# Matrix squarings drained by ScalarE, a gate product and a normalisation moved on GpSimd

## What is computed

```python
ada = silu(c) @ W_ada + b_ada
shift_msa, scale_msa, gate_msa, shift_mlp, scale_mlp, gate_mlp = split(ada, 6)
x = x + gate_msa * attention(modulate(layernorm(x), shift_msa, scale_msa))   # 16 heads of 9
x = x + gate_mlp * (gelu(modulate(layernorm(x), ...) @ W_fc1 + b_fc1) @ W_fc2 + b_fc2)

U, _ = qr(P)                    # P is 144 x 64
A = skew(silu(c) @ W.T + b)     # 64 x 64, one per sequence
R = expm(A)
z = x @ U
x = x + (z @ R - z) @ U.T
```

## Time and profile before

| | |
|---|---|
| median of 3 runs | 378.99 us |
| the profiled execution's own time | 378.52 us |
| its span, first to last instruction | 376.4 us |
| TensorE matmuls busy | 311.6 us, 83% |
| VectorE busy | 245.7 us, 65% |
| ScalarE busy | 144.5 us, 38% |
| GpSimd busy | 118.4 us, 31% |
| mean granted TensorE clock | 0.919 of full speed |

### The profile page before, as it was taken

How to read it: one execution, slowest core, us unless ns; L and a number is a source line. 1 busy time by engine, 2 the same in 40 slices (tenths; PEclk the granted TensorE clock), 3 DMA queues, 4 the chain that set the end, 5 groups by cost and what they waited for, 6 DMA issues and landing times.

```text
span 376.4 us, 7579 instructions
## 1 busy us (share of the span) xinstructions
PE 311.6 (83%) x2645; PEld 187.5 (50%) x2645; DVE 245.7 (65%) x763; ACT 144.5 (38%) x262; POOL 118.4 (31%) x299
## 2 busy tenths in 40 slices
PE   2888966888989789798888887989659999996686
PEld 1333423444444445465554554566536666665456
DVE  6857577676867868879889698764513455545533
ACT  2111112587674734445556364643103233231010
POOL 5812604207016383244270422122160333300000
PEclk9999999998998967989999999999958999997855
DMA  4923321123621212212113000000000000000004
GB/s 120 285 59 98 90 57 31 54 70 73 178 46 46 86 42 58 68 31 65 54 49 93 7 3 3 3 2 0 2 2 0 2 0 2 1 0 2 0 0 125
DMA packets 20202, 17.95 MB, mean 48 GB/s; under 512 B 3524, under 2 KB 18005, under 8 KB 20040
## 3 DMA queue, kind: packets, MB, share of 16 engines
q1 hardware_dynamic: 19556, 16.34, 15.8%
q10 hardware_dynamic: 610, 1.14, 1.0%
HBM read 12.28 MB, written 4.81 MB: 45 GB/s over the span
## 4 chain that ended last, share of the span: by engine, by line
PE 57%; DVE 23%; issue 6%; SPq 4%; ACT 3%; POOL 1%; DMA 0%; DVEq 0%; ACTq 0%; POOLq 0%
DVE nm L914 11%; PE pst L264 10%; PE m L483 6%; PE m L642 6%; PE pst L265 5%; PE ps L449 5%; PE m L286 3%; DVE gp L722 3%; PE m L270 3%; PE pst L470 3%; PE pst L381 3%; SPq L254 2%; DVE gm L723 2%; PE m L264 2%; PE pst L654 2%
## 5 line engine op out<-in xcount | busy, mean ns | idle before, releaser
L914 DVE TENSOR_REDUCE nm<-ps 128x2 f32<-128x512 f32 x128 | 87.6, 688 | 35.3 <-PE ps L449 31.2
L1146 ACT ACTIVATE pex<-pst 128x1024 f32<-128x1024 f32 x64 | 65.6, 1025 | 30.2 <-PE pst L470 29.1
L449 PE MATMUL ps<-ks,qs 54*128 54x256 bf16 x256 | 28.9, 305 | 22.6 <-DVE nm L914 21.9
L751 DVE TENSOR_SCALAR pm<-m 64x1 f32<-64x1 f32 x64 | 13.6, 212 | 45.8 <-PE m L286 45.4
L483 PE MATMUL m<-pex,ve 128*32 128x256 f32 x512 | 37.8, 417 | 0.0
L1458 POOL TENSOR_TENSOR xin<-xin,res 128x288 f32<-128x288 f32 x16 | 12.7, 791 | 71.0 <-DVE res L943 71.0
L270 PE MATMUL m<-gm,ident 64*64 64x65 f32 x126 | 24.4, 282 | 6.9 <-DVE gm L723 3.9
L449 PEld LDWEIGHTS ps<-ks,qs 54*128 54x128 bf16 x256 | 10.9, 101 | 36.3 <-issue 31.2
L286 PE MATMUL m<-qst,ident 64*64 64x64 f32 (+42 forms) x128 | 19.8, 234 | 11.1 <-DVE qst L757 11.1
L470 PE MATMUL pst<-qs,ks 56*128 56x256 bf16 x256 | 27.0, 290 | 1.8 <-DMA qs<-nmT 1.0
L270 PEld LDWEIGHTS m<-gm,ident 64*64 64x64 f32 x126 | 14.3, 159 | 26.9 <-issue 19.6
(11 more groups left out here) (248 smaller groups left out, 574.2 us busy)
## 6 DMA issues: line engine op xcount, KB each, us to landing
scr_qk<-parts SPq DMA_DIRECT2D x24, 144.0 KB, 2.0
qs<-scr_qk SPq DMA_DIRECT2D x96, 36.0 KB
ks<-scr_qk SPq DMA_DIRECT2D x72, 36.0 KB
gates<-scr_ada SPq DMA_DIRECT2D x2, 576.0 KB, 6.3
out_dram<-xin SPq DMA_DIRECT2D x8, 144.0 KB, 1.9
wr<-in_L_cond_W_dram SPq DMA_DIRECT2D x1, 1134.0 KB
xin<-in_x_dram SPq DMA_DIRECT2D x1, 864.0 KB, 5.2
ks<-scr_qk ACTq DMA_DIRECT2D x24, 36.0 KB
```

Of the source, the lines that this page charges most:

```text
L449: ins = mm(ps[e][:, L * i:L * i + L], qs[64 * e:64 * e + KS, b % 3, 2 * g + i, 128 * lt:128 * lt + 128], ks[64 * e:64 * e + KS, b % 3, 2 * ...
L914: nc.vector.tensor_reduce(nm[:, lt, e, 2 * g:2 * g + 2], ps[e][:, :].rearrange("p (h l) -> p h l", h=2), AX.X, ALU.max, negate=True).then_ ...
L1146: nc.scalar.activation(pex[:, n % 4, :, :], pst[0][:, :, :], ACT.Exp, scale=ATT_SCALE).then_inc(s("exp_done"), 1)
```

## The change

Four edits.

- A squaring becomes (E + 2I) E. GpSimd adds 2I, a constant tile, to `ef` and writes `ef2`, which lies in the memory of `qq`; TensorE multiplies `ef2` with `ef`; ScalarE copies the product over `ef`. VectorE has no part in it.
- The squares stand in other slots: (3,7), then slots 0, 3, 6 of turns 4 to 7; the last one stands in turn 1 of the MLP, ahead of the transposition into the same bank.
- The attention's projection is copied out of PSUM by ScalarE (`projected`) in slot 0, for sequences 0 to 5, and GpSimd multiplies it with the gate ahead of its addition to x. Sequences 6 and 7 stay as they were.
- GpSimd normalises input t + 4 at the end of turn t, behind the split, instead of input t + 3 at the start of turn t behind the shift.

```diff
-            for n in ((7,) if t == EXPM else (3, 5, 7) if t < B - 1 else (3, 4, 5, 7)):
+            for n in (7,) if t == EXPM else (0, 3, 6):
                 SQUARES[t, n] = len(SQUARES)
...
             def square(n, bank):
-                pe.wait_ge(s("ef_ready"), n + 1)
+                pe.wait_ge(s("ef2_ready"), n + 1)
...
-                            last = mm(m[half, at:at + R], ef[half, p, 1 - e, :], ef[half, p, e, :], start=True, stop=True)
+                            last = mm(m[half, at:at + R], ef2[half, p, 1 - e, :], ef[half, p, e, :], start=True, stop=True)
...
                     chain(mlp_steps(t, 5))
+                if t == 1:
+                    square(SQUARINGS - 1, 5)
                 if t >= 0 and real(t + 2):
                     transpose_h(B + t + 2, 5)
...
-            def squared(n):
-                m = await_fill(dve, "square", n)
-                ins = nc.vector.scalar_tensor_tensor(out=ef_flat, in0=ef_flat, scalar=2.0, in1=m[:, :], op0=ALU.mult, op1=ALU.add)
-                drained(ins, "square", n)
-                await_drain(dve, "square", n)
-                dve.sem_inc(s("ef_ready"), 1)
...
-                    if n == 0 and real(t - 2):
-                        gated("proj", t - 2, 0, res[:, :, :])
...
-                    if (t, n) in SQUARES:
-                        squared(SQUARES[t, n])
...
+            def squared(n):
+                drained(nc.scalar.copy(ef_flat, await_fill(act, "square", n)[:, :]), "square", n)
+
+            def projected(b):
+                m = await_fill(act, "proj", b)
+                if b:
+                    act.wait_ge(s("x1_ready"), b)
+                drained(nc.scalar.copy(res[:, :, :].rearrange("p t c -> p (t c)"), m[:, 0:LT * C]), "proj", b)
...
+                    if n == 0 and real(t - 2):
+                        projected(t - 2)
...
                     if n == 6 and real(t + 3):
                         evac_qk("qk01", t + 3, 0, 2)
+                    if (t, n) in SQUARES:
+                        squared(SQUARES[t, n])
...
+                if t == 1:
+                    squared(SQUARINGS - 1)
                 if real(t + 2):
                     evac_hT(B + t + 2)
...
+            def gated(b):
+                await_drain(pool, "proj", b)
+                if b == 0:
+                    pool.wait_ge(s("gates_loaded"), 32)
+                then(nc.gpsimd.tensor_tensor(res[:, :, :], res[:, :, :], gates[:, 0, b:b + 1, :].to_broadcast([128, LT, C]), ALU.mult))
+                xb = xin[:, LT * b:LT * b + LT, :]
+                nc.gpsimd.tensor_tensor(xb, xb, res[:, :, :], ALU.add).then_inc(s("x1_ready"), 1)
+
+            def plus_two(n):
+                if n:
+                    await_drain(pool, "square", n - 1)
+                else:
+                    await_drain(pool, "e0", 0)
+                nc.gpsimd.tensor_tensor(ef2[:, :, :, :].rearrange("p b e n -> p (b e) n"), ef[:, :, :, :].rearrange("p b e n -> p (b e) n"),
+                                        two_i[:, :].unsqueeze(1).to_broadcast([2 * R, 2 * BP, R]), ALU.add).then_inc(s("ef2_ready"), 1)
+
+            def plus_two_after(t, n):
+                if (t, n) in SQUARES and SQUARES[t, n] + 1 < SQUARINGS:
+                    plus_two(SQUARES[t, n] + 1)
...
             for t in range(-1, B):
                 if t > 0:
                     shift(t, 1)
-                if t >= 0 and t + 3 < B + 2:
-                    normalise(t + 3)
+                plus_two_after(t, 0)
                 if real(t - 2):
-                    added("proj", t - 2, res[:, :, :], "x1_ready")
+                    gated(t - 2)
+                plus_two_after(t, 3)
                 if t >= 0 and real(t + 1):
                     shift(t + 1, 0)
                 if t == BASIS_TURN:
                     basis_norms()
                 if real(t - 2):
                     mlp_deviations(t - 2)
+                if t == EXPM:
+                    plus_two(0)
+                plus_two_after(t, 6)
                 if t == 2:
                     weight_parts(1, wfc1_b, "mlp_loaded", 96, slice(3 * C, 3 * C + FF))
                 if real(t + 3):
                     split(t + 3)
+                plus_two_after(t, 7)
+                if t + 4 < B + 2:
+                    normalise(t + 4)
```

More of the change, by code:

```diff
@@ L68, in cond_seq_program @@
         below = sb("below", [R, R])
+        two_i = sb("two_i", [2 * R, R])
         onesb = sb("onesb", [3 * H2 * 2, L], BF16)
@@ L114, in cond_seq_program @@
         ef = sb("ef", [2 * R, BP, 2, R])
+        ef2 = qq
         efs = sb("efs", [R, B, R])
@@ L241, in cond_seq_program @@
         for t in range(EXPM, B):
-            for n in ((7,) if t == EXPM else (3, 5, 7) if t < B - 1 else (3, 4, 5, 7)):
+            for n in (7,) if t == EXPM else (0, 3, 6):
                 SQUARES[t, n] = len(SQUARES)
-        assert len(SQUARES) == SQUARINGS
+        assert len(SQUARES) == SQUARINGS - 1
         TURNED = [(0, 7), (1, 6), (2, 5), (3, 5), (4, 5), (6, 5), (7, 5), (7, 6)]
@@ L874, in exponential_of_scaled @@
                 drained(ins, "e0", 0)
-                await_drain(dve, "e0", 0)
-                dve.sem_inc(s("ef_ready"), 1)
-            def squared(n):
-                m = await_fill(dve, "square", n)
-                ins = nc.vector.scalar_tensor_tensor(out=ef_flat, in0=ef_flat, scalar=2.0, in1=m[:, :], op0=ALU.mult, op1=ALU.add)
-                drained(ins, "square", n)
-                await_drain(dve, "square", n)
-                dve.sem_inc(s("ef_ready"), 1)
             def signs():
@@ L894, in signed_exponential @@
             def signed_exponential():
+                await_drain(dve, "square", SQUARINGS - 1)
                 for e in range(2):
@@ L940, in gated @@
                     dve.wait_ge(s("x1_ready" if which == 0 else "x2_ready"), b)
-                elif which == 0:
-                    dve.wait_ge(s("gates_loaded"), 32)
                 ins = nc.vector.tensor_tensor(to, m[:, 0:LT * C].rearrange("p (t c) -> p t c", t=LT),
@@ L1165, in channels @@
                 drained(nc.scalar.copy(oTb[:, :], m[0:CB + 1, L:2 * L]), "oc", t)
+            ef_flat = ef[:, :, :, :].rearrange("p b e n -> p (b e n)")
+            def squared(n):
[5 more added lines that the diff above has]
+                drained(nc.scalar.copy(res[:, :, :].rearrange("p t c -> p (t c)"), m[:, 0:LT * C]), "proj", b)
             def turn_a(t):
@@ L1509, in _ @@
                                         pattern=[[0, BP], [-1, R]], channel_multiplier=1).then_inc(s("half_ready"), 1)
+            nc.gpsimd.memset(two_i[:, :], 0.0).then_inc(s("two_ready"), 1)
+            for i in range(2):
+                pool.wait_ge(s("two_ready"), i + 1)
+                nc.gpsimd.affine_select(out=two_i[:, :], in_=two_i[:, :], compare_op=ALU.not_equal, fill=2.0, base=-R * i,
+                                        pattern=[[-1, R]], channel_multiplier=1).then_inc(s("two_ready"), 1)
+            pool.wait_ge(s("two_ready"), 3)
             for t in range(-1, B):
```

## The result

The kernel after takes 396.31 us (median of 4 runs, 393.43 to 398.15) against 379.15 (378.2 to 379.45) for the kernel before on the same chip: ratio 1.0463, 95% interval 1.0411 to 1.0515. It is slower, as forecast, but by 17.2 us where 8.2 were forecast, and 396.3 lies above the range. The profiled execution took 398.15 us, 396.4 of it span, at a mean granted clock of 0.888 (0.919 before). Some executions of a kernel take over 1.5% longer than its fastest, at a lower mean clock; the medians here are over all executions, the ratios leave those out.

What follows compares the result with a forecast made beforehand. Neither TensorE nor VectorE was full; GpSimd's margins ahead of TensorE's shift transposition (1.56 to 2.22 us) decide. Terms 2.4 + 2.4 + 2.9 + 1.6 - 1.0 - 1.2 - 0.8 + 1.95 = +8.2 us gave 387; range 380 to 392.5.

Steps and rivals of the forecast that it cites:

- 2.4 + 2.4 + 2.9 + 1.6 = 9.3: TensorE's waits for GpSimd's delayed shift, in us: ends of turns 0 to 2 together, then of turns 3, 4 and 5.
- about 10%: Expected share of GpSimd in the chain of work that ended last, up from 1%.
- The gate's product: Moving six gate products from VectorE to GpSimd was credited no gain, and their time on GpSimd was taken as hidden.
- The wait of 0.86 for nmT: Slot 5 of turn 4: the square's wait for bank 5, held by the shift's copy, was to be gone.
- Rival B: VectorE held off by GpSimd's two-input additions and products: +3 us, 390; chance 0.12.
- Rivals C: C: half of the turn-end costs vanish in existing waits, 9.3 becomes 4.7: 382.5 us; chance 0.12.
- rival D: TensorE reaches the shift's transposition no earlier than GpSimd delivers, stalls vanish, only the squares' terms stand: -2.5, 376.5 us; chance 0.10.
- rival A: TensorE's stops in slot 1 bring three more falls of the granted clock: +4 us, 391; chance 0.14.
- Term 1.95: Last square in the MLP's turn 1: 1.08 us of its own plus a wait of 0.87 for its copy.
- Terms -1.0, -1.2 and -0.8: Gains in us from the attention's squares in their new slots, in turns 4, 6 and 7.
- -1.4 for turn 5: Gain in us of turn 5 from the squares, counted only if its end has no stall.

Runs made afterwards that it cites:

- gate_only: The kernel before with the gate's product alone moved (ScalarE copies the projection, GpSimd multiplies): 377.93 us, ratio 1.0015 to the kernel before.
- norm_back: The kernel after with GpSimd's normalisation put back behind the shift, all else as changed: 384.53 us, ratio 1.0155 to the kernel before.
- last_early: norm_back with the last square one MLP turn sooner, in turn 0: 380.12 us, ratio 1.0038 to the kernel before.
- fill: The kernel after with twelve unread matmuls ahead of the wait for the shift in slot 1, 84 in all: 387.86 us, ratio 1.0279 to the kernel before.
- slots_only: The kernel before with only the squares' slots new, VectorE still combining: 381.15 us, ratio 1.0084.
- last_early_warm: last_early with the filler matmuls of warm: 372.8 us, ratio 0.9862 to the kernel before.
- warm: The kernel before with 36 unread matmuls in the MLP's turn 0 and six per chain gap in its last two turns: 372.05 us, ratio 0.9869.
- squares_only: The kernel before with the squares alone changed (ScalarE's copy, GpSimd's addition, new slots): 384.65 us, ratio 1.0107.
- after_warm: The kernel after with all fillers, those of fill and warm and eight in the MLP's turn 1: 384.4 us, ratio 1.015 to the kernel before.
- norm_only: The kernel before with GpSimd's normalisation alone moved ahead of the next shift: 389.03 us against 378.22, one of 4 runs at 382.06.

## Why the prediction was off by half

**Right.** GpSimd's order was the cause, and the place was as forecast: six waits in slot 1, 10.3 us in sum where 2.4 + 2.4 + 2.9 + 1.6 = 9.3 was the forecast, the longest 2.81. That the sums agree is partly luck: the first three waits make 5.1 us for 2.4, the last three 5.2 for 6.9. The chain's share of GpSimd came out at 12% for "about 10%". The gate's product costs nothing (gate_only). The wait of 0.86 for nmT is gone, slot 5 of turn 4 went from 4.19 to 2.12 us. Rival B fell: L728's mean did not move. Rivals C and D fell too: six waits of 10.3 us stand there, and undoing the normalisation gives 11.8 us, so nothing was absorbed. An addition takes 1.268 us, inside its bounds. (The Trainium skill, "GPSIMD Engine Reference", section "Elementwise — side-by-side cycle accounting", scaled down to 512 elements, would have given an estimate of 1.12; the measurement decides.)

**The step that failed: the granted clock taken as it was.** The sum prices waits and moved work and puts the clock at nothing. In the profiles TensorE's rest grew by 8.6 us, close to the forecast's 8.2; the other 11.4 us are its same 2645 matmuls taking longer. Of the 11.4, 3.6 go with the normalisation (after to norm_back), 3.5 with the last square (to last_early), and 4.3 stay with the squares in the attention. That fill gets 8.4 us back net, though GpSimd is no sooner in the place shown, says the same. This is rival A, to which the forecast gave 0.14, argued from turns 4 to 7 having run at 1.00 in the kernel before. That was evidence from one execution of a stream without these stops. Its price was also read too low: turn 2 of the earlier trace rows touches three falls and not two, and the low clock grew by 27.8 us, not by three falls of 4. (The Trainium skill, "TensorE: Matmul & The Clock Gate", section "HAM oscillation", says that waits for DMA which recur in a loop bring the low clock back each time. Here the waits are for GpSimd, and three of the six have a fall at them and three have not.)

**The turn ends: the mechanism right, the size nearly.** The forecast's kernel without the stops is rival D's, 376.5; with them 387.2. That prices the normalisation at 10.7 us, and norm_back measures 11.8. In the profiles the parts are off in opposite directions: 7.5 us of rest where 10.7 were priced, and 3.6 of slower matmuls that had no term.

**The last square: sized at less than half.** Term 1.95, measured 4.4 (norm_back to last_early). Its own time and its copy, 1.14 and 0.69, were in the sum; the second wait of 0.68 and the low clock behind both were not.

**The squares in the attention: the wrong sign, and the largest miss.** Terms -1.0, -1.2 and -0.8, with rival D's -1.4 for turn 5 -4.4; measured +1.6 in all by last_early, which has the other two costs taken out. The step that failed is the one that priced slots 5 to 7 and took the squares of slot 0 as free. In turn 4 the gain of slot 5 was larger than forecast (2.06 for 1.1), but the square in slot 0 pays its own 1.08 and a wait of 1.04 for an addition queued behind the split, and slots 6 and 7 together lost 1.07. The -1.2 of turn 6 became +2.1: slot 0 lost 1.9, and slot 6 ran at the low clock. Why it fell there is open, since slots_only has the longer wait and no fall. Turn 7's -0.8 came, as -0.6. Nor is it the clock alone: last_early_warm is no faster than warm.

Against the forecast, then: 1.1 us short on the turn ends, 2.4 on the last square, 6.0 on the squares in the attention. The three measured steps, 11.8 + 4.4 + 1.6 = 17.8, are one chain of differences from the kernel after to the kernel before. That they come to the measured 17.2, within the 0.6 by which the kernel before differs between the chips, follows from this and proves nothing.

**Open.** How much of the 11.8 is clock: 3.6 us by one pair of profiles, and what the fillers give back, 5.4 to 8.4, is in part clock that the stops had not taken. Where the clock falls differs between executions of one kernel, so single turns can't be attributed; squares_only ran from 379.19 to 385.1. after_warm has 92 fillers more than last_early_warm, whose own cost was not run apart: if it is above nothing, the two pieces cost that much less than the 11.6.

## What to carry to other kernels

On an engine that works in order, a long operation moved ahead of a short one has to be priced against the short one's margin, which is read as the time from the end of the producer to the start of the consumer in the trace of before. A stop of 1 to 3 us on TensorE can then cost more than its length, since the work behind it may run at half speed: here 11.8 us for waits of 10.3 in sum (norm_back), and 10.8 for 8.1 by norm_only's median, but 3.8 in its one execution with a high clock. And moved work has to be priced in the slot that it moves to, not only in the one that it leaves: the squares in slot 0 turned a forecast gain into a small loss. Where such a stop can't be avoided, matmuls that nobody reads, issued ahead of the wait and shorter than it, are worth a try.

## What was not expected

- Filling idle time made the kernel before 6.5 us faster (378.51 to 372.05) with more work in it, 2741 matmuls for 2645.
- The low clock grew from 60.8 to 88.6 us though no stop for the shift lasts over 2.81 us, and the same matmuls took 11.4 us more of busy time, which is more than the stops themselves.
- The fillers cost 5 us where TensorE did not wait, 84 of 0.124 us each (1.49 / 12), 10.4 us in sum. Little of that was hidden: the rest of the span grew by 8.1 us, and the kernel's own matmuls, 4.1 us shorter at a higher clock, paid for the difference.
